# Building one-hot matrices: three wide comparisons and products in place of one wide and eight narrow ones, and a shorter digit sum

## The reference

```
h = relu(layernorm(x));  e = dis[dst] * dis[src]          # dis = degree ** -0.5
10 times: agg = segment_sum(feat[src] * e, dst)
          feat = r[i] * (0.9 * agg + 0.1 * h) + (1 - r[i]) * feat
x = x + feat
h = relu(layernorm(x))
4 times:  m = (h @ W_msg.T + b_msg).reshape(n, 4, 128)
          r = segment_sum(m[src, edge_type], dst);  h = GRU(r, h)
x = x + h
```

## Time and profile before

| | us |
|---|---|
| median of three runs | 2552.06 |
| the profiled execution, its own time | 2550.86 |
| its span (first to last instruction) | 2549.3 |
| busy in the span: PE, DVE, ACT, POOL | 2190.8, 1488.7, 335.0, 134.9 |
| the stage of the change, 63.5 to 521.2 | 457.7 |

### The profile page before, as it was taken

The page is one execution under the profiler, slowest core; times in us unless marked ns, Lnnn a source line. Parts: engine busy times, 40 slices in busy tenths (PEclk is TensorE's granted clock), DMA queues, the critical chain, the costliest instruction groups (busy, mean ns, idle before and its releaser), DMA issues.

```text
span 2549.3 us, 41289 instructions
## 1 busy us (share of the span) xinstructions
PE 2190.8 (86%) x14375; PEld 1440.7 (57%) x14886; DVE 1488.7 (58%) x3473; ACT 335.0 (13%) x494; POOL 134.9 (5%) x391
## 2 busy tenths in 40 slices
PE   1544545559999999999799999999999999999996
PEld 1322333348999898988644455444554446544464
DVE  6988999977777777777662234522444324442243
ACT  0322223330000000000121011210112100220000
POOL 1322222200000000000000000000000000000000
PEclk9996555559999999999899999999999999999998
DMA  2000000010000000001400000000000000000001
GB/s 72 21 21 21 21 21 21 28 41 2 1 2 2 2 2 2 1 2 49 139 1 1 1 1 1 1 1 1 1 1 1 1 1 1 1 1 1 1 1 50
DMA packets 22188, 34.32 MB, mean 13 GB/s; under 512 B 2450, under 2 KB 18442, under 8 KB 21469
## 3 DMA queue, kind: packets, MB, share of 16 engines
q1 hardware_dynamic: 19025, 30.56, 3.5%
q10 hardware_dynamic: 2944, 0.93, 0.2%
HBM read 18.04 MB, written 13.45 MB: 12 GB/s over the span
## 4 chain that ended last, share of the span: by engine, by line
PE 75%; DVE 15%; issue 5%; DVEq 2%; DMA 2%; ACT 0%; POOLq 0%; ACTq 0%; POOL 0%
PE ps L787 41%; PE ps L706 26%; DVE hot_pair L967 8%; PE ps L739 3%; PE ps L727 2%; DVEq L961 2%; DVE dig L990 1%; DVE hot_place L964 1%; DVE big L993 1%; DMA big<-in_L_gnn_w_hh 1%; PE ps L647 1%; DMA x_after_hops<-x 1%; PE ps L691 1%; PE ps L605 1%; DVE dig L992 1%
## 5 line engine op out<-in xcount | busy, mean ns | idle before, releaser
L787 PE MATMUL ps<-slots,m_parts 125*128 125x500 fp8e4 (+1 forms) x5600 | 1088.0, 354 | 6.6 <-DVE m_parts L1337 5.2
L787 PEld LDWEIGHTS ps<-slots,m_parts 125*128 125x128 f16 x5600 | 547.4, 98 | 495.7 <-issue 10.0
L706 PE MATMUL ps<-parts,big 125*128 125x256 f16 x6125 | 669.6, 273 | 6.8 <-issue 4.2
L706 PEld LDWEIGHTS ps<-parts,big 125*128 125x128 fp8e4 x6125 | 591.3, 98 | 63.6
L605 PE MATMUL ps<-hot_pair,hot_place 125*128 125x228 f16 x1000 | 230.6, 400 | 256.5 <-DVE hot_pair L967 256.5
L1255 DVE TENSOR_SCALAR slots<-big 128x3200 int32<-128x3200 int32 (+1 forms) x112 | 244.1, 2183 | 279.8 <-PE ps L787 279.7
L605 PEld LDWEIGHTS ps<-hot_pair,hot_place 125*128 125x128 f16 x1000 | 143.1, 149 | 343.8 <-DVE hot_pair L967 283.1
L967 DVE TENSOR_SCALAR hot_pair<-iota_pair,win 125x228 f16<-125x228 f16 x1000 | 262.5, 334 | 3.1 <-issue 3.1
L1357 DVE SCALAR_TENSOR_TENSOR r_parts<-ps,over,r_parts 128x500 f16<-128x500 f32 (+1 forms) x28 | 19.1, 684 | 230.1 <-ACT r_parts L527 230.1
L1364 DVE SCALAR_TENSOR_TENSOR gate_r<-ps,over,gate_r 128x500 f32<-128x500 f32 (+1 forms) x28 | 19.1, 682 | 229.3 <-PE ps L739 221.8
L1183 DVE SCALAR_TENSOR_TENSOR hop_tmp<-ps,coef,g 125x128 f32<-125x128 f32 x250 | 87.6, 350 | 97.9 <-PE ps L706 94.4
(11 more groups left out here) (200 smaller groups left out, 1130.2 us busy)
## 6 DMA issues: line engine op xcount, KB each, us to landing
packed_counts<-packed SPq DMA_DIRECT2D x16, 625.0 KB, 3.3
big<-packed_counts SPq DMA_DIRECT2D x4, 1600.0 KB, 7.3
big<-packed_counts SPq DMA_DIRECT2D x3, 1200.0 KB, 6.5
hd<-in_x SPq DMA_DIRECT2D x1, 1562.5 KB
x_again<-in_x SPq DMA_DIRECT2D x1, 1562.5 KB
x_after_hops<-x SPq DMA_DIRECT2D x1, 1562.5 KB
big<-x_after_hops SPq DMA_DIRECT2D x1, 1562.5 KB
out<-big SPq DMA_DIRECT2D x4, 250.0 KB
```

Source lines behind the costliest of these rows:

```text
L706: last = pe.matmul(ps[:, n % RING, 0:2 * F], tot_f8[0:Q, c, a, :], both((parts0, parts1)[par], a), start=a == 0, stop=a == TILES - 1)
L787: last = pe.matmul(ps[:, k % 2, 0:SIZES[k] * Q], m_parts[0:Q, a, h, t * F:(t + 1) * F], slots_f8[0:Q, t % 2, 0:SIZES[k], a, 0:Q], start=a ...
```

## The change

1. `onehots`: three TENSOR_TENSOR operations a group. `marks` (8 rows of 128, row by row) compares a row 0..127 with each chunk's place; `hot_pair` (8 rows of 228) compares a row 0..227 with each chunk's key; `weighed` multiplies `marks` by the weights. So that the innermost run has two neighbouring elements in every operand, keys, places and weights are staged twice each (`[.., W, 2]`, float16), and rows are seen as pairs. The third operation waits for the first by a semaphore. The weights move from `hot_pair` to the places' matrix; TensorE loads `weighed[:, w, :]`, contiguous.
2. Buffers for four groups (`DEPTH`) instead of two. GpSimd's `stage_window` waits for TensorE's use of the buffer (`s_hot_used`), no longer for VectorE's building, and writes 125x16 elements in each of its three operations; its loop holds four windows.
3. TensorE waits for a whole group (`s_pairs`, `s_weighed_d`) instead of for each w.
4. `sum_digits`: five operations; the last three become one multiplication by 17/16 on uint16 (adds each value to itself shifted by four) and one masking that writes straight to `big1`. It now stands before the last group of each block, not after the fourth, and for block 14 behind the last group of all.
5. ScalarE's `part_lane` is spread: the three lane copies of a block go between the evacuations of the next block's first groups.
6. Keys step by 456 for each group (`KQ`), so that they are exact in float16 near zero; the general branch converts back. GpSimd makes one more row of constants (`iota_row`) at the start.

```diff
@@ -49,13 +49,17 @@
 LO, MANY, LOWBITS = 0, QB, 0x03030303
 LANES, LANE = 3, 9
 KP = 228
-KQ = 1024
+KQ = 456
+KG = 1024
+NOWHERE = -4096.0
+DEPTH = 4
+ROUND = 2
 
 
 class Chain:
...
             win_p = sb("win_p", [128, 2, W], F16, b)
             win_x = sb("win_x", [128, 3], F32, b)
-            hot_pair = sb("hot_pair", [128, 2, W, KP], F16, b)
...
+            hot_pair = sb("hot_pair", [128, DEPTH, W, KP], F16, b)
+            marks = sb("marks", [128, DEPTH, W, 128], F16, b)
+            weighed = sb("weighed", [128, DEPTH, W, 128], F16, b)
         with ExitStack() as b:
...
+            def stage_window(q, b):
+                lo = pool.value_load(windows[0:1, ds(q, 1)], min_val=0, max_val=NCH)
+                pool.wait_ge(s_hot_used, q + 1)
+
+                def twice(m):
+                    return m.rearrange("p (w o) -> p w o", o=1).broadcast_to([CH, W, 2])
+
+                pool.tensor_copy(win_place[0:CH, b, :, :], twice(tab[0:CH, 0, ds(lo, W)]))
+                pool.tensor_copy(win_f[0:CH, b, :, :], twice(tab[0:CH, 1, ds(lo, W)]))
+                pool.tensor_tensor(win_key[0:CH, b, :, :], twice(keys[0:CH, ds(lo, W)]),
+                                   q_off[0:CH, ds(q, 1)].rearrange("p (w o) -> p w o", o=1).broadcast_to([CH, W, 2]),
+                                   ALU.subtract).then_inc(s_wst, 1)
+
+            with pool.Fori(0, Q // DEPTH) as i:
+                for j in range(DEPTH):
+                    stage_window(DEPTH * i + j, j)
+            for q in range(Q // DEPTH * DEPTH, Q):
+                stage_window(q, q % DEPTH)
...
 
             def evacuate(blk, b, j):
                 q = BQ * blk + j
-                act.wait_ge(s_hot_used, W * q + 3 * W)
+                act.wait_ge(s_hot_used, q + 1 + DEPTH)
                 summed(q, extras, s_more_used)
+                if j == 0:
+                    act.wait_ge(s_bytes, blk + 1)
                 act.activation(words[:, b, :, j], ps[:, j, 0:KP], ACT.Copy, scale=float(ONE)).then_inc(s_taken, 1)
 
-            def part_lanes(blk, turn, b, last):
-                act.wait_ge(s_taken, last + 1 + BANKS)
-                act.wait_ge(s_digits, blk + 1)
-                act.wait_ge(s_packed[b], 16 * turn + 16)
+            def part_lane(turn, b, l, last):
+                blk = 2 * turn + b
+                if l == 0:
+                    act.wait_ge(s_taken, last + 1 + BANKS)
+                    act.wait_ge(s_digits, blk + 1)
+                    act.wait_ge(s_packed[b], 16 * turn + 16)
                 lanes = words[:, b, :, :].bitcast(U8).rearrange("p n (q l) -> p (n q) l", l=4)
-                for l in range(LANES):
-                    n = min(LANE, TILES - l * LANE) * TILES * BQ
-                    at = l * LANE * TILES * BQ
-                    ins = act.activation(packed[:, b, at:at + n], lanes[:, 0:n, l], ACT.Copy)
-                ins.then_inc(s_bytes, 1)
-
-            def block_of(turn, b, n):
+                n = min(LANE, TILES - l * LANE) * TILES * BQ
+                at = l * LANE * TILES * BQ
+                ins = act.activation(packed[:, b, at:at + n], lanes[:, 0:n, l], ACT.Copy)
+                if l == LANES - 1:
+                    ins.then_inc(s_bytes, 1)
+
+            def block_of(turn, b, n, turn_before):
                 blk = 2 * turn + b
-                act.wait_ge(s_bytes, blk + 1)
                 for j in range(n):
-                    evacuate(blk, b, j)
-                part_lanes(blk, turn, b, BQ * blk + n - 1)
-
-            with act.Fori(0, NB // 2 - 1) as i:
-                block_of(i, 0, BQ)
-                block_of(i, 1, BQ)
-            block_of(NB // 2 - 1, 0, BQ)
-            block_of(NB // 2 - 1, 1, Q - (NB - 1) * BQ)
+                    if j >= 2:
+                        evacuate(blk, b, j - 2)
+                    elif turn_before is not None:
+                        evacuate(2 * turn_before + 1 - b, 1 - b, BQ - 2 + j)
+                    if 3 <= j < 3 + LANES and turn_before is not None:
+                        part_lane(turn_before, 1 - b, j - 3, 16 * turn_before + BQ * (1 - b) + BQ - 1)
+
+            block_of(0, 0, BQ, None)
+            with act.Fori(0, (NB - 2) // ROUND) as i:
+                for k in range(ROUND // 2):
+                    turn = ROUND // 2 * i + k
+                    block_of(turn, 1, BQ, turn)
+                    block_of(turn + 1, 0, BQ, turn)
+            for turn in range((NB - 2) // ROUND * ROUND // 2, NB // 2 - 1):
+                block_of(turn, 1, BQ, turn)
+                block_of(turn + 1, 0, BQ, turn)
+            block_of(NB // 2 - 1, 1, Q - (NB - 1) * BQ, NB // 2 - 1)
+            evacuate(NB - 1, 1, 3)
+            part_lane(NB // 2 - 1, 0, 2, BQ * (NB - 1) - 1)
+            evacuate(NB - 1, 1, 4)
+            for l in range(LANES):
+                part_lane(NB // 2 - 1, 1, l, Q - 1)
...
-            pe.sem_inc(s_hot_used, 2 * W)
+            pe.sem_inc(s_hot_used, DEPTH)
...
             def count(q, b, j):
 
                 pe.wait_ge(s_taken, q + 1)
+                pe.wait_ge(s_pairs, q + 1)
                 for w in range(W):
-                    pe.wait_ge(s_hot, W * q + w + 2 * W + 1)
-                    pe.matmul(ps[:, j, 0:KP], hot_place[0:CH, b, :, w], hot_pair[0:CH, b, w, :],
-                              start=w == 0, stop=w == W - 1, skip_group_check=True).then_inc(s_hot_used, 1)
+                    if w == 0:
+                        pe.wait_ge(s_weighed_d, q + 1)
+                    last = pe.matmul(ps[:, j, 0:KP], weighed[0:CH, b, w, :], hot_pair[0:CH, b, w, :],
+                                     start=w == 0, stop=w == W - 1, skip_group_check=True)
+                last.then_inc(s_hot_used, 1)
...
-            with pe.Fori(0, NB - 1) as i:
-                for j in range(BQ):
-                    count(BQ * i + j, j % 2, j)
-            for j in range(Q - (NB - 1) * BQ):
-                count(BQ * (NB - 1) + j, j % 2, j)
+            PER_TURN = BQ * ROUND // 2
+            with pe.Fori(0, Q // PER_TURN) as i:
+                for j in range(PER_TURN):
+                    count(PER_TURN * i + j, j % DEPTH, j % BANKS)
+            for q in range(Q // PER_TURN * PER_TURN, Q):
+                count(q, q % DEPTH, q % BANKS)
...
                 many = dve.value_load(windows[0:1, ds(q + MANY, 1)], min_val=0, max_val=NCH)
                 dve.wait_ge(s_wst, q + 1)
-                dve.wait_ge(s_hot_used, W * q + W)
-                TT(hot_place[0:CH, b, :, :], iota_place[0:CH, :, :],
-                   win_p[0:CH, b:b + 1, :].broadcast_to([CH, 128, W]), ALU.is_equal)
-                for w in range(W):
-                    TS(hot_pair[0:CH, b, w, :], iota_pair[0:CH, :], win[0:CH, b, 0, w:w + 1],
-                       win[0:CH, b, 1, w:w + 1], ALU.is_equal, ALU.mult).then_inc(s_hot, 1)
+                dve.wait_ge(s_hot_used, q + 1)
+
+                def by_two(m, n):
+                    return m.rearrange("p w (n two) -> p w n two", two=2)
+
+                def row(m, count, n):
+                    return m.rearrange("p (o n two) -> p o n two", o=1, two=2).broadcast_to([CH, count, n // 2, 2])
+
+                def each(m, count, n):
+                    return m.rearrange("p w (o two) -> p w o two", o=1).broadcast_to([CH, count, n // 2, 2])
+
+                TT(by_two(marks[0:CH, b, :, :], 128), row(iota_row[0:CH, :], W, 128),
+                   each(win_place[0:CH, b, :, :], W, 128), ALU.is_equal).then_inc(s_marks, 1)
+                TT(by_two(hot_pair[0:CH, b, :, :], KP), row(iota_pair[0:CH, :], W, KP),
+                   each(win_key[0:CH, b, :, :], W, KP), ALU.is_equal).then_inc(s_pairs, 1)
+                dve.wait_ge(s_marks, q + 1)
+                TT(by_two(weighed[0:CH, b, :, :], 128), by_two(marks[0:CH, b, :, :], 128),
+                   each(win_f[0:CH, b, :, :], W, 128), ALU.mult).then_inc(s_weighed_d, 1)
...
             def sum_digits(blk, b):
 
                 dve.wait_ge(s_bytes, blk + 3)
-                x, low, high, lower = packed[:, b, :].bitcast(I32), dig[:, 0, :], dig[:, 1, :], dig[:, 2, :]
-                u16 = [d.bitcast(DT.uint16) for d in (low, high, lower)]
+                x, low, high = packed[:, b, :].bitcast(I32), dig[:, 0, :], dig[:, 1, :]
+                low16, high16 = low.bitcast(DT.uint16), high.bitcast(DT.uint16)
                 TS(low, x, TWOS, None, ALU.bitwise_and)
                 step(TS(high, x, 2, TWOS, ALU.logical_shift_right, ALU.bitwise_and))
-                step(TT(u16[0], u16[0], u16[1], ALU.add))
-                TS(high, low, NIBBLES, None, ALU.bitwise_and)
-                step(TS(lower, low, 4, NIBBLES, ALU.logical_shift_right, ALU.bitwise_and))
-                step(TT(big1[:, :].bitcast(DT.uint16).rearrange("p (n q) -> p n q", q=64)[:, :, ds(4 * blk, 4)],
-                        u16[1].rearrange("p (n q) -> p n q", q=4), u16[2].rearrange("p (n q) -> p n q", q=4), ALU.add))
+                step(TT(low16, low16, high16, ALU.add))
```

(33 more changed lines are left out.)

31 lines of the change are left out of this document (20 added, 11 removed).

## The result

The changed kernel takes 2486.14 us (median of 4 runs, 2485.12 to 2489.36) where the kernel before takes 2553.34 on the same chip (4 runs, 2551.03 to 2561.13): a ratio of 0.973, with a 95% interval of 0.971 to 0.976. That is 67 us less, where 72 were forecast. The forecast of 2480 is 6 us too low. The sum hits, but one of its terms came out at half its size and another was nil, and the stages that the forecast left alone became 7 us shorter; part of the hit is luck. Its own sign of being wrong, a stage that isn't about 385 us long, did come: the stage is 400.4 us long.

The account below looks back on a forecast made before the run. VectorE was taken to bound the one-hot stage. Savings of 45, 24 and 5 us less 2 make 72, from 2550.86 to 2479, with the median 1.2 above: 2480 us; range 2463 to 2530.

Parts of the forecast that it names:

- A: One-hots on VectorE: three wide operations make a group 2.26 us instead of 2.62, saving 45 us over 125 groups.
- B: Digit sum on VectorE: cheaper multiplication and masking save 1.50 us a block, 24 us over 16.
- C: Turn of VectorE's loop: a group issued between covers part of the stand, 3.9 instead of 4.58 us, saving 5 us.
- D: Tail: block 14's digit sum behind the last group makes VectorE stand for ScalarE's lane copies, costing 2 us.
- What bounds the kernel: One-hot stage: VectorE bounds it, so what the change does to VectorE's time there passes to the end one for one.
- The wait inside the group: VectorE's third operation waits for the first, but its instruction stream is ready 0.4 us early: price 0.
- second stall: A further 0.45 us stand of VectorE where the loop turns, counted within the 3.9 us of a turn.
- Rival 1: GpSimd's staging must wait for a gap in VectorE, 0.45 us in affected groups: 2515 us, or 2536; chance 0.31.
- Rival 2: Runs of two elements lose VectorE's fast path: groups of 4.34 us, 215 us slower, 2740 in all; chance 0.08.
- Rival 3: TensorE's period, 2.20 us at best, becomes 2.45 and bounds the groups, costing 24 us: 2504; chance 0.12.

Follow-up runs that it names:

- the third experiment: Changed kernel with per-chunk operands read as one element again and again (innermost step 0) instead of stored pairs: 2729.3 us, ratio 1.069.
- The last experiment: Changed kernel with masking split into 624 rows and one, ROUND = 14, and block 14's digit sum behind the layer-norm statistics: 2452.42 us, ratio 0.961.
- The filler: Changed kernel with 56 instructions (long-fulfilled waits) put in TensorE's program ahead of the counting: 2505.12 us, ratio 0.981.
- the kernel without turns: Changed kernel with ROUND = 14 instead of 2, all 14 blocks written out in one body: 2461.82 us, ratio 0.964.
- the digit sum alone: Kernel before the change with only the new digit sum body, at its old place: 2543.56 us, ratio 0.995.
- even rows: Changed kernel with each digit sum's masking cut in two operations, 624 rows and the last row alone: 2478.95 us, ratio 0.971.
- six operations: Changed kernel with three more small GpSimd copies for each window, six instead of three: 2510.56 us, ratio 0.983.

## Why the prediction was right, term by term, and where it wasn't

A is 125 groups. B is 14 sums in the loop that add 6.47 us to a block where they added 7.23, the 15th in the tail (5.6 for 7.2), and 0.7 for the last, behind the statistics. C is what is left of the stage's 57.2 us and the 0.7 behind it.

| term | forecast | measured |
|---|---|---|
| A, the one-hots | 45 | 47.5 |
| B, the digit sum | 24 | 12.9 |
| C, the turn of the loop | 5 | -0.4 |
| D, the tail | -2 | -2.0 |
| behind the degree matmuls | 0 | -3.5 |
| rounds and message steps | 0 | 10.5 |
| sum | 72 | 65.0 |

The changed stage and its tail gave 58 us, 14 less than the 72 of the forecast, and so the stage is 400.4 us long and not about 385. The total is off by only 7 because the stages that the forecast put at nothing gave the other 7; that part is luck.

**What bounds the kernel: right.** VectorE's time in the stage passed to the end; nothing else came late in its place.

**A: right.** The group is 2.237 us long (2.26 forecast) against 2.617 on average before, 0.380 x 125 = 47.5. The slope taken from an operation of another type held. The runs of two cost nothing, and the third experiment shows that this was no matter of course: with runs of one the group is 4.26. The wait inside the group, costed at nothing, doesn't show.

**B: the mechanism was right, the masking's size was off.** The failed step is "the masking is like L992, 0.80; its scattered runs cost L993 nothing". L992 has the same type and number of elements, but it writes in one piece. L993 has the scatter, but two sources and 1.46 us: its layout in a one-source operation had never been seen. The masking measured 1.456, which is 0.65 us x 16 = 10 of the 11 us missing; beside it the gap ahead of the masking is 0.14 us where 0.03 was taken, and the other pieces nearly balance. The multiplication, for which the text gave bounds of 0.81, 1.47 and 2.80, was right at 0.82; the masking, for which it gave no bounds, was wrong.

**C: wrong.** From start to start, over a plain group and a plain sum, a turn cost 3.4 to 3.6 us before and costs 3.4 to 3.7 after. The step added 0.88 us to the branch, 2.91 of standing and 0.85 to the next comparison, took off the group's 2.26, got 2.4, and put 0.45 of a second stall on top. In the chain of the turn the group starts at 180.28 and the loop line is through at 181.67, 1.39 us in; the stream goes on at 184.97, 3.30 later; the comparison starts at 185.97, 1.00 later. That is 5.69, less 2.24. The second stall is gone, but each of the three pieces is longer than was taken, the branch most of all (0.5 us): everything that a group issues lies ahead of it, the wait for `marks` too. The stand itself is 0.4 us longer than the 2.91 of before; why, no run shows. So the group does cover part of the stand, as the step has it, but only its last 0.92 us and not 1.38. There are six turns, not seven: together they gave 0.2 us, and the one group with a ninth chunk lost 0.4 (1.39 us on top, 1.02 before).

**D: right.** VectorE's timeline behind the last group:

```profile
455.64 0.68 DVE L1029 TENSOR_TENSOR weighed<-marks,win_f 125x1024 f16<-125x1024 f16 x1
458.35 0.81 DVE L1050 TENSOR_SCALAR dig<-packed 128x1250 int32<-128x1250 int32 x1 [2.04 <-ACT packed L504]
...
463.94 4.93 DVE L1111 BATCH_NORM_STATS2 stat_x<-hd 125x6 f32<-125x128 f32 x25 [0.22 <-DVE big L1054]
```

2.04 us for ScalarE's lane copy. The last experiment shows that they could be had back.

**Outside the terms.** "All later stages run on TensorE and read `big1`, which stays as it is; I leave them alone" was wrong by 7 us. The filler shows for the message steps that TensorE's instructions ahead of them are the cause. What in them matters (where the code comes to lie, or how far the stream is ahead of the engine) isn't shown; their mere number is not it, as the kernel without turns has many more and the short steps. The 3.5 us behind the degree matmuls are not settled. VectorE there waits behind a branch on the degree flag:

```profile
497.82 0.18 DVE L1222 TENSOR_REDUCE w_max<-deg 125x1 f32<-125x25 f32 x1 [3.72 <-issue]
```

Before, the same idle time was 1.25 us, at the same operation; that is 2.5 of the 3.5 us. From the end of the degree matmuls to the first round are 7.9 us before and 11.35 after. Four of the other kernels have 8.2 (the filler), 9.4 (no turn), 11.05 (the digit sum alone) and 11.2 (even rows). It moves with the code and not with the work. The filler's kernel has 3.47 us of idle time at that operation too and still a short way to the first round, so more than one stand is in it.

**Rival 1** had its mechanism right and its condition wrong. GpSimd gets through at an end of a VectorE operation too, not only in gaps, and three operations have three ends. The price it named, 0.45 us a group, is about the one that six operations cost in a group that has to wait. **Rival 2** exists at its price with runs of one; the doubled staging avoids it. **Rival 3** was not seen: TensorE waits for VectorE 124 times and VectorE for TensorE not once. GpSimd does wait for TensorE's matmuls, 92 times, which the prediction named as a sign of this rival; but with four buffers it gets through in time, and with two VectorE feels it.

## What to carry to other kernels

Before an operation is priced from a row of another one, check that the row could have shown the difference: a two-source operation says nothing of what a layout does to a one-source operation, where an odd number of rows took 1.8 times as long (1456 ns against 819). Beside a VectorE with no gaps, count GpSimd's operations against the ends of VectorE's: one for each end was free here, and three more cost almost half a microsecond in each group that had to wait. Price the turns of a loop with the distance at which the branch is reached, and allow a measured change some 10 us of this span for stages that it never touched, since changed instruction streams shift the stands of later code.

## What the runs showed of the hardware that was not expected

- An int32 TENSOR_SCALAR that writes 625 rows of two from a contiguous source takes 1456 ns; 624 rows take 819, and the last row 161 more. Beside the 625 rows GpSimd's operations take 0.2 us, beside the 624 rows 0.77.
- GpSimd, beside back-to-back two-source operations, completes at most one operation at each end, 0.04 to 0.08 us behind it (263 such ends in the changed kernel's stage); in a stand it does one in 0.2 us.
- VectorE's stream stands for 2.9 to 3.3 us when the loop turns, and TensorE's for 1.6 to 2.2 at the start of a gather or not at all, depending on instructions about a millisecond earlier in its program: 56 of them moved four message steps from 1241.6 to 1251.8 us, while 56 groups more, written out, left them at 1241.7.
